# A mixture of experts in 64x64 tiles, with routing over sixteen rounds and its normalisation shared with the next stage

## The chip, the cores and the metric

The kernel runs on one core of one Trainium2 chip. The metric is the device time of one execution in microseconds, the median of several runs.

## The reference

The kernel computes a small language model tower on a batch of 32 sequences of 512 tokens with 64 features: spectral token features, neighbourhood attention, a mixture of experts, a decayed (linear) attention, and a second, softly routed mixture. The change touches the first mixture:

```python
def _moe(tokens, router_w, w1, b1, w2, b2):
    logits = tokens @ router_w.T
    probs = jax.nn.softmax(logits, axis=-1)
    rw, re = jax.lax.top_k(probs, TOP_K)                  # 2 of 8
    rw = rw / jnp.maximum(rw.sum(-1, keepdims=True), 1e-12)
    combine = zeros((N, E)).at[arange(N)[:, None], re].set(rw)
    out = tokens
    for e in range(E):
        h = jax.nn.gelu(tokens @ w1[e] + b1[e], approximate=False)
        y = h @ w2[e] + b2[e]
        out = out + combine[:, e:e + 1] * y
    return out
```

Between the stages the kernel applies the residual and a normalisation over the features (a variance, Ln and Exp for the reciprocal root, and a product).

## The kernel before, in words

**Layout.** Two sequences form a pair: 16 pairs, 64 features of each sequence on 64 of the 128 partitions, 512 tokens along the free axis. `s.h` holds the residual stream, `s.z` the normalised input of a stage. Every stage is a block in which each of the five engines has its own program; they meet at semaphores, and at a barrier between the blocks. Inside a block, `unrolled(count, unroll, (lead, stage), ...)` writes out an engine's order: in iteration n it issues each stage in the order given, for step n + lead.

**The mixture, `mixture_of_experts`.** There are 64 steps: 16 pairs by 4 pairs of experts (`ep`). A step has these parts:

- `first` on TensorE: the four products of two experts by two sequences, 64x64 each, into `p_1` (two PSUM banks).
- `gelu` on ScalarE: one activation of 1024 columns into `g` (two buffers).
- `expand` on TensorE: a 0/1 matrix `s.pick` spreads the routing weights of the step over the partitions of `p_c`, in fp32r and two 32x128 tiles. The weights are held as a high and a low part.
- `weigh` on VectorE: `gw = p_c * g`, 1024 columns.
- `second` on TensorE: two products 128x64 (both experts contracted at once) accumulated into `p_y[slot]`, one bank per pair, with a fp32r bias product at the pair's first step.
- After a pair's last step `residual` on VectorE adds the kept input, and GpSimd adds that into `s.h` and squares it.

TensorE's order per iteration is (4, first), (3, expand), (2, second), (6, turn), (20, logits_of), (0, spreads); ScalarE's is (4, gelu), (6, fetch), (20, router), (0, deviations).

**Routing.** Four pairs are routed together (`router`, once in 16 steps): `logits_of` makes the logits and transposes them into `p_r`, some 20 small VectorE operations follow one another (each waits for the one before) at steps 1 to 7 of the 16, then `turn` transposes the weights into `p_t` and `fetch` copies them to `ct`. For the first group this chain stands ahead of all rounds.

**Normalisation for the next stage.** `spreads` (variance of four pairs, into `p_r`, at step 14 of 16) and `deviations` (copy out; Ln and Exp for three groups together at the third, for the last alone at the end). Then `hop` writes the result to DRAM, `spread` broadcasts a row of it to 64 partitions by two DMAs per pair, and `scaled` on GpSimd makes `s.z`. Of the 16 pairs 12 are scaled at the end of the mixture's block, the last four at the start of `decayed_attention`, which also fetches each pair's halves swapped by two DMAs from SyncE (`fetch`) before it can project. In `decayed_attention` the variances of the following normalisation are made in the bank of the outputs, `p_y`; `outputs` of steps 5, 9 and 13 wait for the Exp that reads it. At the start of the mixture GpSimd scales four pairs, too, before its loop.

**Tables.** ScalarE's function tables are loaded where a function is not in the current set, or ahead with `preload_act_table_set`. The mixture and decayed attention have no such preload.

## Time and profile before

| | |
|---|---|
| median of 3 runs | 962.57 us (961.24 to 964.74) |
| the profiled execution, its own time | 959.21 us |
| its span, first to last instruction | 957.4 us |
| mean granted TensorE clock | 0.931 |
| busy: TensorE products, weight loads | 827.2 us (86%), 414.7 us (43%) |
| busy: VectorE, ScalarE, GpSimd | 570.5 us (60%), 469.8 us (49%), 289.2 us (30%) |
| first mixture, first routing product to barrier | about 390 to 607 us |
| decayed attention | about 607 to 735 us |

PE is TensorE, PEld its weight loads, DVE is VectorE, ACT is ScalarE, POOL is GpSimd, SP is SyncE; q behind an engine means its queue. The start of a row is its time from the start of the span. A row with xN is N instructions merged. Ends of matmuls are modelled, so for TensorE the distance between the starts of neighbouring groups says more than their duration. What stands in brackets is how long the engine was idle before, and which instruction released it. Four f32 products appear as x8, as each is two instructions.

### The profile page before, as it was taken

What the parts mean: (1) busy time and instruction counts of PE and PEld (TensorE: products, weight loads), DVE (VectorE), ACT (ScalarE), POOL (GpSimd) and SP (SyncE); (2) the same over time, 40 slices, a digit from 0 to 9 for tenths busy, and PEclk for the clock granted to TensorE, in tenths of its full rate; (3) what the DMA queues carried; (4) which work ended last, traced back from release to release, by engine and by line L of the source; (5) the groups of instructions that cost most, each with busy time, mean ns of one, the idle gap of its engine ahead of it and who ended that gap; (6) DMA issues with size and microseconds to landing.
All of it is one profiled execution on the core that took longest, in us unless ns stands there. A gap on an engine that the chain in (4) does not pass through costs nothing. (4 is left out here: it accounts for less than half of the span.)

```text
span 957.4 us, 28793 instructions
## 1 busy us (share of the span) xinstructions
PE 827.2 (86%) x12656; PEld 414.7 (43%) x12656; DVE 570.5 (60%) x831; ACT 469.8 (49%) x579; POOL 289.2 (30%) x286
## 2 busy tenths in 40 slices
PE   4796799999999987299999979298886599999996
PEld 2231477767767765022222212176663333333332
DVE  5446477757766765475857525086653147777776
ACT  2243476767767775154444453223332155555553
POOL 4034735334353431311222206533444160000000
PEclk9899799999999999699999979599988689999998
DMA  4200310010010010100000022312322101121110
GB/s 90 31 14 32 97 43 27 4 58 4 4 59 4 4 59 4 55 1 1 1 1 1 1 66 87 101 45 67 89 76 82 26 17 46 56 56 46 45 45 34
DMA packets 39775, 37.81 MB, mean 39 GB/s; under 512 B 21025, under 2 KB 25282, under 8 KB 39650
## 3 DMA queue, kind: packets, MB, share of 16 engines
q1 hardware_dynamic: 38578, 34.35, 12.8%
q8 instruction: 101, 1.65, 0.7%
q10 hardware_dynamic: 1072, 1.60, 0.5%
q14 instruction: 24, 0.20, 0.1%
HBM read 19.95 MB, written 7.60 MB: 29 GB/s over the span
## 5 line engine op out<-in xcount | busy, mean ns | idle before, releaser
L1914 ACT ACTIVATE se_a<-se_p,cols 128x512 f32<-128x512 f32 x128 | 92.7, 774 | 77.5 <-PE se_p L1867 77.5
L1191 DVE TENSOR_REDUCE na_rowmax<-na_ps 128x16 f32<-128x1024 f32 x64 | 78.1, 1220 | 76.8 <-PE na_ps L1067 76.8
L1483 DVE TENSOR_TENSOR me_gw<-me_pc,me_g 128x1024 f32<-128x1024 f32 x64 | 78.3, 1223 | 73.9 <-PE me_pc L1338 69.3
L1934 DVE SCALAR_TENSOR_TENSOR se_a<-se_p,cols,z 128x1024 f32<-128x1024 f32 x64 | 82.2, 1284 | 61.9 <-PE se_p L1877 61.9
L1379 ACT ACTIVATE me_g<-me_p,cols 128x1024 f32<-128x1024 f32 x64 | 71.3, 1114 | 83.9 <-PE me_p L1326 79.2
L925 POOL TENSOR_TENSOR z<-na_k,const 128x512 f32<-128x512 f32 x64 | 64.6, 1042 | 140.7 <-ACT na_k L1131 140.7
L496 POOL TENSOR_TENSOR n_sq<-h 128x512 f32<-128x512 f32 x64 | 68.6, 1077 | 110.3 <-DVE h L848 43.2
L531 POOL TENSOR_TENSOR z<-h,n_bc 128x512 f32<-128x512 f32 x62 | 78.4, 1280 | 24.4 <-DMA n_bc<-n_spread 24.3
L1194 DVE TENSOR_TENSOR na_e<-na_ps,na_rowmax 128x1024 f32<-128x1024 f32 x64 | 78.4, 1225 | 2.2
L1326 PE MATMUL me_p<-z,moe_w 64*64 64x512 f32 x512 | 72.4, 636 | 6.6 <-ACT me_g L1379 6.6
L1867 PE MATMUL se_p<-z,f_w 64*64 64x512 f32 x256 | 70.5, 618 | 4.9 <-DMA se_zswap<-z 4.0
L1076 PE MATMUL na_pt<-const,na_e 128*128 128x128 f32 x512 | 69.2, 278 | 2.3 <-ACT na_et L1161 1.7
L1348 PE MATMUL me_py<-me_gw,w_out 128*64 128x512 f32 x256 | 69.9, 625 | 0.4 <-DVE me_gw L1483 0.4
L1161 ACT ACTIVATE na_et<-na_pt 128x1024 f32<-128x1024 f32 x64 | 65.5, 1024 | 7.7 <-PE na_pt L1076 6.8
L1867 PE MATMUL se_p<-se_zswap,f_w 64*64 64x512 f32 x256 | 69.1, 618 | 0.0
L1877 PE MATMUL se_p<-se_a,f_w 64*64 64x512 f32 x512 | 68.3, 600 | 0.6 <-DVE se_a L1934 0.6
L1154 ACT ACTIVATE na_e<-na_e 128x1024 f32<-128x1024 f32 x64 | 67.3, 1054 | 1.3 <-DVE na_e L1194 0.9
L1889 PE MATMUL se_py<-se_a,w_out 64*64 64x512 f32 x512 | 67.3, 589 | 0.5 <-DVE se_a L1934 0.5
L1265 POOL TENSOR_TENSOR h<-h,me_added 128x512 f32<-128x512 f32 x16 | 20.7, 1292 | 151.7 <-DVE me_added L1491 151.7
L1076 PEld LDWEIGHTS na_pt<-const,na_e 128*128 128x128 f32 x512 | 56.0, 140 | 13.8 <-issue 10.8
L1148 ACT ACTIVATE na_v<-na_pm 64x512 f32<-64x512 f32 x64 | 38.6, 604 | 33.2 <-PE na_pm L1027 32.8
L1067 PE MATMUL na_ps<-z,na_q 32*32 32x256 f32 x2048 | 52.9, 397 | 0.6 <-issue 0.6
(288 smaller groups left out, 1322.0 us busy)
## 6 DMA issues: line engine op xcount, KB each, us to landing
n_bc<-n_spread SPq DMA_DIRECT2D x128, 128.0 KB, 3.0
da_zswap<-z SPq DMA_DIRECT2D x32, 128.0 KB, 2.4
se_zswap<-z SPq DMA_DIRECT2D x32, 128.0 KB, 2.3
out<-se_rows SPq DMA_DIRECT2D x16, 256.0 KB, 2.1
n_spread<-n_rstd SPq DMA_DIRECT2D x13, 256.0 KB, 2.0
const<-in_const ACTq DMA_DIRECT2D x1, 712.0 KB, 6.4
const<-in_const ACTq DMA_DIRECT2D x1, 562.0 KB, 4.0
f_w<-in_L_ffn_W SPq DMA_DIRECT2D x4, 128.0 KB
```

The source lines that it names most:

```text
L496: return nc.gpsimd.tensor_tensor(s.sq[p % 8][:], row(s.h, p), row(s.h, p), ALU.mult)
L531: return eng.tensor_tensor(row(s.z, p), row(s.h, p), s.bc[p % 4][:], ALU.mult)
L1076: mm = nc.tensor.transpose(p_t[:, c, :], e[b][:, 2 * c:2 * c + 2, :].rearrange("p h w -> p (h w)"), const(s, "ident"))
L1191: nc.vector.tensor_reduce(rowmax[b][:], scored, AX, ALU.max).then_inc(s_max, 1)
L1194: nc.vector.tensor_tensor(e[b][:], scored, rowmax[b][:].unsqueeze(2).broadcast_to([128, GROUPS, WIN]), ALU.subtract).then_inc(s_diff, 1)
L1326: mm = nc.tensor.matmul(p_1[half[e2], b, :], s.moe_w1[half[b], 2 * ep + e2, :], row(s.z, at.of(4))[half[b], :], start=True, stop=True, ski ...
L1348: mm = nc.tensor.matmul(p_y[slot][half[b], :], s.moe_w2[:, ep, :], gw[at.k % 2][:, b, :], start=False, stop=(ep == EP - 1), skip_group_che ...
L1379: nc.scalar.activation(g[at.k % 2][:], p_1[:], ACT.Gelu, bias=col(s, "moe_b1", ep)).then_inc(s_g, 1)
L1483: nc.vector.tensor_tensor(gw[at.k % 2][:], p_c[:], g[at.k % 2][:], ALU.mult).then_inc(s_gw, 1)
L1867: mm = nc.tensor.matmul(hidden(at.n, e2)[half[b], :], s.f1_w1[half[e2], 2 * ep + e2, :], z[half[e2], :], start=True, stop=True, skip_group ...
L1914: nc.scalar.activation(a1[at.k % 2][:, e2, :], hidden(at.n, e2)[:], ACT.Relu, scale=col(s, "f1_g1", 2 * ep + e2), bias=col(s, "f1_be1", 2 ...
L1934: nc.vector.scalar_tensor_tensor(out=a2[at.k % 2][:], in0=p_2[:], scalar=col(s, "f1_be2", ep), in1=s.f1_w[:, ep, :].unsqueeze(1).broadcast ...
```

## The change

In the mixture:

- `first` is unchanged in its products, but writes into three single banks (`hidden(n, b)`), 6 steps ahead instead of 4. `gelu` becomes two activations of 512 columns per step, into four buffers that lie in free rows of `s.z`.
- `expand` becomes four 64x64 products in bf16. For this the routing weights are split into three bf16 parts (high, middle, rest) instead of two, and the constant `pick` is twice as wide.
- `second` becomes four 64x64 products in f32 into two banks, one for the even, one for the odd experts; the bias becomes two 64x64 f32 products. A pair's end therefore has two parts: `residual` on VectorE for the first bank, `fetch_odd` on ScalarE, a copy of the second, and two additions on GpSimd.
- `p_t` is gone; the turned weights go through `p_r`, and `fetch` copies them twice (bf16 and f32).
- Routing is spread over steps 2 to 15 of the 16 and starts 24 steps ahead instead of 20. GpSimd scales the four pairs left over from before one at a time in its loop.
- The variances stand at steps 17, 33 and 49 instead of 14, 30, 46 and 62. At step 33 Ln and Exp of groups 0 and 1 are made, and their eight pairs are scaled inside the mixture. Swapped halves of pairs 0 and 1 are fetched there. Groups 2 and 3 (variance of the last, Ln, Exp, hops, eight spreads and scalings) move into `decayed_attention`, the variance, Ln and Exp at its start, the spreads and scalings into its first four steps (`former`).
- Both blocks preload a table on ScalarE. The low and high parts of the bias in f32r and the five GpSimd operations that made them are gone.

```diff
-    s.pick = sb("pick_r", [128, EP, 128], F32R)
+    s.pick = sb("pick_b", [128, 2, EP, 128], BF16)
...
+def fetch_swapped(sp, s, p):
+    half = [slice(0, 64), slice(64, 128)]
+    for x in range(2):
+        sp.dma_start(s.swapped[p % 2][half[x], :], row(s.z, p)[half[1 - x], :]).then_inc(s.n_swapped[p % 2], 16)
...
-        p_1, p_c, p_y, p_t, p_r = ps("p1", [128, 2, T])[0], ps("pc", [128, 2, T])[0], ps("py", [128, T], 2), ps("pt", [128, T])[0], ps("pr", [128, T])[0]
+        p_1, p_c, p_y, p_r = ps("p1", [128, T], 3), ps("pc", [128, 2, T])[0], ps("py", [128, 2, T])[0], ps("pr", [128, T])[0]
...
+        def hidden(n, b):
+            return p_1[(2 * n + b) % 3]
...
             def first(at):
-                te.wait_ge(s_g, done(at.n - 1))
+                te.wait_ge(s_g, done(2 * at.n - 2))
...
             def expand(at):
                 te.wait_ge(s_gw, done(at.n - 1))
                 for b in range(2):
-                    rows = slice((2 * slot + b) * ROUTES, (2 * slot + b + 1) * ROUTES)
-                    mm = nc.tensor.matmul(p_c[:, b, :], s.pick[rows, ep, :], routes[rows, :], start=True, stop=True, skip_group_check=True)
+                    for e2 in range(2):
+                        mm = nc.tensor.matmul(p_c[half[e2], b, :], s.pick[half[b], slot, ep, half[e2]], routes[half[b], :],
+                                              start=True, stop=True, skip_group_check=True)
...
             def second(at):
+                if ep == 0:
+                    te.wait_ge(s_even, done(at.of(4) - 1))
+                    te.wait_ge(s_odd, done(at.of(4) - 1))
+                    for b in range(2):
+                        nc.tensor.matmul(p_y[half[b], b, :], s.moe_b2[half[b], slot, :], routes[half[b], :], start=True, stop=False, skip_group_check=True)
                 te.wait_ge(s_gw, done(at.n))
-                for b in range(2):
-                    mm = nc.tensor.matmul(p_y[slot][half[b], :], s.moe_w2[:, ep, :], gw[at.k % 2][:, b, :], start=False, stop=(ep == EP - 1),
-                                          skip_group_check=True)
+                for e2 in range(2):
+                    for b in range(2):
+                        mm = nc.tensor.matmul(p_y[half[b], e2, :], s.moe_w2[half[e2], ep, :], gw[at.k % 2][half[e2], b, :],
+                                              start=(ep == 0 and b != e2), stop=(ep == EP - 1), skip_group_check=True)
...
-            unrolled(EP * NP, 16, (4, first), (3, expand), (2, second), (6, turn), (20, logits_of), (0, spreads))
+            unrolled(EP * NP, 16, (4, turn), (6, first), (3, expand), (2, second), (AHEAD, logits_of), (0, spreads))
...
+            sc.preload_act_table_set("gelu_and_others")
...
             def gelu(at):
-                sc.wait_ge(s_gw, done(at.n - 2))
-                nc.scalar.activation(g[at.k % 2][:], p_1[:], ACT.Gelu, bias=col(s, "moe_b1", ep)).then_inc(s_g, 1)
+                sc.wait_ge(s_gw, done(at.n - 4))
+                for b in range(2):
+                    nc.scalar.activation(g[at.n % 4][:, b, :], hidden(at.n, b)[:], ACT.Gelu, bias=col(s, "moe_b1", ep)).then_inc(s_g, 1)
+
+            def fetch_odd(at):
+                slot, ep = where(at)
+                if ep == EP - 1:
+                    i = at.of(4)
+                    sc.wait_ge(s_w2, done(at.n))
+                    sc.wait_ge(s_hz, done(2 * (i - 2) + 1))
+                    nc.scalar.activation(odd[slot][:], p_y[:, 1, :], ACT.Copy).then_inc(s_odd, 1)
...
-            unrolled(EP * NP, 16, (4, gelu), (6, fetch), (20, router), (0, deviations))
+            unrolled(EP * NP, 16, (2, fetch_odd), (4, fetch), (6, gelu), (AHEAD, router), (0, deviations))
...
         @block.scalar
         def _(sc):
+            sc.preload_act_table_set("natural_log_exp_and_others")
             give_credits(sc, s_qkd)
+
+            def former():
+                sc.wait_ge(s.n_var, quad(2, LAST))
+                nc.scalar.activation(s.rstd[:, 2, :], s.rstd[:, 2, :], ACT.Ln, bias=s.eps[:])
+                nc.scalar.activation(s.rstd[:, LAST, :], p_y[:], ACT.Ln, bias=s.eps[:]).then_inc(s.n_ln, 1)
+                sc.wait_ge(s.n_ln, 7)
+                nc.scalar.activation(s.rstd[:, 2:4, :], s.rstd[:, 2:4, :], ACT.Exp, scale=-0.5).then_inc(s.n_rstd, 2)
```

## Rows read from the trace of the kernel before

**Rows 1.** Timeline, a steady mixture round: start us, duration, engine, line, [idle before <-releaser]

```profile
436.25 1.09 PE L1326 MATMUL me_p<-z,moe_w 64*64 64x512 f32 x8
...
437.27 0.49 PE L1338 MATMUL me_pc<-me_ct,pick_r 32*128 32x512 f32 x2
437.41 1.11 ACT L1379 ACTIVATE me_g<-me_p,cols 128x1024 f32<-128x1024 f32 x1 [1.34 <-PE me_p L1326]
...
437.70 1.08 PE L1348 MATMUL me_py<-me_gw,w_out 128*64 128x512 f32 x4
437.87 1.23 DVE L1483 TENSOR_TENSOR me_gw<-me_pc,me_g 128x1024 f32<-128x1024 f32 x1 [1.23 <-PE me_pc L1338]
...
438.71 1.09 PE L1326 MATMUL me_p<-z,moe_w 64*64 64x512 f32 x8
```

**Rows 2.** Timeline, a pair's end in the last stage

```profile
837.45 1.05 PE L1877 MATMUL se_p<-se_a,f_w 64*64 64x512 f32 x8
...
838.31 1.06 PE L1889 MATMUL se_py<-se_a,w_out 64*64 64x512 f32 x8
...
839.42 0.60 ACT L1922 ACTIVATE se_odd<-se_py 128x512 f32<-128x512 f32 x1 [0.27 <-PE se_py L1889]
...
841.87 0.75 PE L1900 MATMUL se_pt<-const,se_res 128*128 128x128 f32 x4
```

**Rows 3.** Timeline, TensorE alone, window mask of the neighbourhood attention

```profile
237.63 0.43 PE L1061 MATMUL na_ps<-winmask_b,ident_b 32*32 32x512 bf16 x16
237.85 0.40 PE L1067 MATMUL na_ps<-z,na_q 32*32 32x256 f32 x8
```

**Rows 4.** Timeline, start of the mixture: VectorE's slowest, first transpose, first second product

```profile
395.87 1.44 DVE L1435 TENSOR_TENSOR me_best<-me_best,const 128x256 f32<-128x256 f32 x1
...
405.62 1.12 PE L1317 MATMUL me_pt<-const,me_ctin 128*128 128x128 f32 x4 [11.33 <-DVEq L1477]
...
413.79 1.08 PE L1348 MATMUL me_py<-me_gw,w_out 128*64 128x512 f32 x4
```

**Rows 5.** Timeline, around the deviations of three groups

```profile
552.26 1.58 ACT L1396 ACTIVATE n_rstd<-n_rstd,eps 128x1536 f32<-128x1536 f32 x1
...
559.17 1.99 PE L1326 MATMUL me_p<-z,moe_w 64*64 64x512 f32 x8 [6.44 <-ACT me_g L1379]
```

**Rows 6.** Timeline, the seam between mixture and decayed attention

```profile
595.87 1.08 PE L1348 MATMUL me_py<-me_gw,w_out 128*64 128x512 f32 x4 [0.37 <-DVE me_gw L1483]
...
597.83 1.26 POOL L1265 TENSOR_TENSOR h<-h,me_added 128x512 f32<-128x512 f32 x1 [0.90 <-DVE me_added L1491]
...
599.17 1.04 POOL L496 TENSOR_TENSOR n_sq<-h 128x512 f32<-128x512 f32 x1
...
606.21 0.63 ACT L1398 ACTIVATE n_rstd<-n_rstd 128x512 f32<-128x512 f32 x1
...
607.59 0.42 POOL L1561 MEMSET da_state<- 128x384 f32 x1 [2.48 <-POOLq L1223]
...
617.28 1.11 PE L1602 MATMUL da_pqk<-z,w_in 64*64 64x512 f32 x1 [15.08 <-DMA da_zswap<-z]
```

**Rows 7.** Timeline, decayed attention: queries on ScalarE; variance and outputs on TensorE

```profile
652.04 0.69 ACT L1662 ACTIVATE da_q<-da_pqk,cols 128x512 f32<-128x512 f32 x1 [4.32 <-PE da_pqk L1602]
...
663.59 0.69 ACT L1662 ACTIVATE da_q<-da_pqk,cols 128x512 f32<-128x512 f32 x1 [6.33 <-PE da_pqk L1602]
...
669.18 0.69 ACT L1662 ACTIVATE da_q<-da_pqk,cols 128x512 f32<-128x512 f32 x1 [4.33 <-PE da_pqk L1602]
...
708.49 0.69 ACT L1662 ACTIVATE da_q<-da_pqk,cols 128x512 f32<-128x512 f32 x1 [4.32 <-PE da_pqk L1602]
...
721.01 0.69 ACT L1662 ACTIVATE da_q<-da_pqk,cols 128x512 f32<-128x512 f32 x1 [7.31 <-PE da_pqk L1602]
...
653.00 1.07 PE L503 MATMUL da_py<-n_sq,const 128*32 128x512 f32 x8
657.40 1.47 PE L1634 MATMUL da_py<-da_sm,da_v 128*64 128x128 f32 x16 [3.33 <-ACT n_rstd L1670]
```

More of the change, by code:

```diff
@@ L179, in allocate @@
         "sq", "var", "ln", "rstd", "z", "zero", "hop0", "hop1", "hop2", "hop3")]
+    s.swapped = [s.z[:, NB - 2 + n, :] for n in range(2)]
+    s.n_swapped = [ctx.enter_context(nc.semaphore(f"n_s_swapped{n}")) for n in range(2)]
     s.n_bc = [ctx.enter_context(nc.semaphore(f"n_s_bc{k}")) for k in range(4)]
@@ L250, in later_loads @@
         loads.append((s.raw_bo[n:n + 1, :, :], a["L1_ffn_bo"].rearrange("(p two) d -> two p d", two=2)[e2:e2 + 1]))
-        for pair in range(2):
+        for slot in range(2):
             for part in range(3):
-                r = (2 * pair + e2) * ROUTES + part * NE
-                loads.append((s.raw_moe_b2[r:r + NE, e2, :], a["L0_ffn_b2"]))
+                r = (2 * e2 + slot) * ROUTES + part * NE
+                loads.append((s.moe_b2[r:r + NE, slot, :], a["L0_ffn_b2"]))
         first = (2 * D, D)[e2]
@@ L1153, in stage @@
                     sc.wait_ge(s_diff, done(2 * at.n + b))
[L1154 removed]
+                    nc.scalar.activation(e[b], e[b], ACT.Exp, scale=float(DH) ** -0.5).then_inc(s_e, 1)
                 return stage
@@ L1269, in after @@
                 square(nc, s, p).then_inc(s.n_sq, 1)
-                if p >= 13:
-                    for m in range(4 * (p - 13), 4 * (p - 13) + 4):
-                        pool.wait_ge(s.n_bc[m % 4], spread_done(2, m))
-                        scaled(nc.gpsimd, s, m).then_inc(s.n_z, 1)
             unrolled(NP, 2, (0, after))
@@ L1312, in turn @@
                 if at.k % 8 == 0:
[L1313 to L1318 removed]
+                    c, part = at.of(16), at.k // 8
+                    te.wait_ge(s_ctin, done(c))
+                    if part == 0 and c < LAST:
+                        te.wait_ge(s_route, linked_to(c + 1, 1))
+                    else:
+                        te.wait_ge(s_ct, done(2 * c + part - 1))
+                    if part == 1 and c > 0:
+                        te.wait_ge(s_copied, done(c - 1))
+                    for t in range(4):
+                        mm = nc.tensor.transpose(p_r[:, t * 128:t * 128 + 128], ct_in[:, t, part, :, :, :].rearrange("p b j n -> p (b j n)"), const(s, "ident"))
                     mm.then_inc(s_t, 1)
@@ L1530, in fetch, with former @@
             def fetch(at):
-                k, z = at.k, row(s.z, at.n)
-                sp.wait_ge(s_qk, done(at.n - 2))
-                sp.wait_ge(s.n_z, nth(2, at.n))
-                for x in range(2):
-                    sp.dma_start(swapped[k][half[x], :], z[half[1 - x], :]).then_inc(s_zin[k], 16)
+                if at.n >= 2:
+                    sp.wait_ge(s_qk, done(at.n - 2))
+                    sp.wait_ge(s.n_z, nth(2, at.n))
+                    fetch_swapped(sp, s, at.n)
+            def former(at):
+                if at.n < 4:
+                    for p in (8 + 2 * at.n, 9 + 2 * at.n):
+                        if p == 8:
+                            sp.wait_ge(s.n_rstd, quad(2, LAST))
+                            for n in (2, 3):
+                                hop(sp, s, 2, n)
+                        if p % 4 == 0:
+                            sp.wait_ge(s.n_hop[p // 4], hop_done(2, p // 4))
+                        sp.wait_ge(s.n_z, nth(2, p - 4))
+                        spread(sp, s, 2, p, p // 4)
             def normal(p):
@@ L1548, in after @@
                     normal(at.n - 5)
-            sp.wait_ge(s.n_hop[LAST], hop_done(2, LAST))
-            for p in range(4 * LAST, NP):
-                sp.wait_ge(s.n_z, nth(2, p - 4))
-                spread(sp, s, 2, p, LAST)
-            unrolled(NP, 2, (3, fetch), (0, after))
+            unrolled(NP, 2, (2, fetch), (0, former), (0, after))
             normal(NP - 5)
@@ L1562, in _ @@
             give_credits(pool, s_qd)
-            for p in range(NP - 4, NP):
-                pool.wait_ge(s.n_bc[p % 4], spread_done(2, p))
-                scaled(nc.gpsimd, s, p).then_inc(s.n_z, 1)
             def decayed_queries(at):
@@ L1585, in normal, with former @@
                 scaled(nc.gpsimd, s, p).then_inc(s.n_z, 1)
-            unrolled(NP, 2, (1, decayed_queries), (0, after))
+            def former(at):
+                if at.n < 4:
+                    for p in (8 + 2 * at.n, 9 + 2 * at.n):
+                        pool.wait_ge(s.n_bc[p % 4], spread_done(2, p))
+                        scaled(nc.gpsimd, s, p).then_inc(s.n_z, 1)
+            unrolled(NP, 2, (1, decayed_queries), (0, former), (0, after))
             normal(NP - 6)
```

207 lines of the change are left out of this document (111 added, 96 removed).

## The prediction, as put on record before the result

> **What bounds the kernel now.** I read four views in turn: busy time by stretch, to find the stage that the change rewrites (expert mixture, 390 to 607 us, then decayed attention, 607 to 735); the timeline of one steady round; the waits; and the timeline of the seam between the two stages.
>
> In a steady round TensorE is never free. The first product starts at 436.25, the expansion 1.02 later, the second product 0.43 after that, the next round 1.01 after that: 2.46 us [rows 1]. ScalarE's gelu (1.11) and VectorE's product (1.23) end in time. So only fewer TensorE microseconds, or fewer holes, help here. The same four 64x64 products cost 0.86 where the neighbouring groups are 64x64 too (837.45 to 838.31) [rows 2]; 0.16 of each 1.02 belongs to the change of tile shape. The Trainium skill says so too (TensorEngine Tiling (Array Packing), Key Properties: a change of tiling mode drains the array).
>
> The holes are elsewhere: before the rounds (first transpose at 405.62 behind the routing chain), at the deviations (6.44 idle, then the lower of the two clock levels, 1.2 of 2.4 GHz, a group busy 1.99 instead of 1.09), at the seam (second product 595.87, next projection 617.28, 21.41 us), and at three deviations inside decayed attention [rows 4 to 7].
>
> **The change, part by part.** The sum is made against the profiled execution: span 957.4, its own time 959.2. That is 3.4 below the median of the runs, 962.6, so I carry the difference over to the median.
>
> *A round.* First and second product 0.86 each. The expansion, now bf16 in four 64x64 tiles, streams 512 columns once. The nearest row is the window mask, 16 bf16 tiles of 512 columns, which gives the array up after 0.22 (237.63 to 237.85) [rows 3]. Its upper bound is today's 0.43. I take 0.22, since tile shape no longer changes. Round 1.94. Can the others follow? A first product starting at F reaches gelu at F+1.16 (436.25 to 437.41) [rows 1]; a 512-column activation with a bias takes 0.69 [rows 7]; so the next first product may start at F+1.91. It fits by 0.03. VectorE: expansion to product at most 0.60, then 1.23, under 1.94.
>
> *The copy of the odd half.* Each pair's last second product (start S) is followed on ScalarE by a copy of the second bank. In program order it stands in the same iteration as that product and ahead of a gelu whose first half frees the bank for the next first product. The neighbouring stage's twin starts 1.11 after its product and takes 0.60 [rows 2]. So the gelu's half starts at S+1.71 and ends at S+2.40, and the first product goes at S+2.45 instead of S+0.86: 1.59 idle, for the 14 pairs that still have a first product to come. Queued behind the copy is gelu, behind gelu all of TensorE. A pair is 4 x 1.94 + 0.86 (the bias, f32 now and priced like a group of f32 tiles; if its two tiles overlap the next ones, half of that) + 1.59 = 10.2, against 4 x 2.46 + 0.43 = 10.3 before. The tiles gain 2.1 a pair and the copy and bias take it back.
>
> *Start.* The chain of 20 small VectorE operations runs to 405.5 while GpSimd scales four tiles; three two-input operations are stretched beyond their quiet 0.42, the worst to 1.44 [rows 4], together by 2.5. GpSimd now scales only one tile then. The three-part split adds about 0.5. First transpose at about 403.6: -2.0. Then two copies instead of one (+0.6), but gelu's table is already there and two first products are already made; second product 6.9 after the transpose instead of 8.17: -1.3.
>
> *Second product 0 to 63, before 182.1.* After: 1.7 for the first with its bias; 59 full iterations 114.5; 15 biases 12.9; seven transposes of weights at 0.84 (0.75 busy [rows 2] and a drain) 5.9; two routing products 2.1 (variances and the other transposes fall in the copy's holes); the holes 14 x 1.59 = 22.3; the tail, where no first product covers VectorE, 5.5. The Ln and Exp of two groups still need three table loads: two thirds of Ln's 1.58 and of a like Exp, the copy and the gelu leave TensorE idle 5.2, and then 3.1 are lost at half clock as today after 6.44 [rows 5]: 8.3. Sum 173.2. For routing operations that meet GpSimd's longer work I add 1.5 (between 0 and 10). 174.7: -7.4.
>
> *Seam, before 21.41.* GpSimd starts 1.96 after the last second product; two additions at 1.34 and a square 1.04 end at 5.7; the barrier costs 0.75 (606.84 to 607.59) [rows 6]. The last variance follows, at half clock 1.8, then the projection, whose swapped halves and scaled rows are there: 8.2. Ln, Exp, hop and eight broadcasts are no longer ahead of it: -13.2. What now stands beside the first four pairs: SyncE's 16 broadcasts, GpSimd's two scalings per pair (at 1.26 like its additions, 2.5 of a 5.59 period), ScalarE's Ln and Exp before its first fetch (0.7 late, given back as the variance takes part of the half-clock stretch). I cost these at nothing; without cover they would cost up to 2.5 a pair, 10.
>
> *Decayed attention.* Period 5.59 (663.59 to 669.18), but 11.55 and 12.52 where deviations are made (first and last of three) [rows 7]. TensorE waits 3.33 for Exp and then runs slow. With one table for both, outputs start 1.1 (product to ScalarE, as 436.25 to 437.41) + 0.7 (Ln, like the 0.69) + 0.63 (Exp) + 0.1 = 2.54 after the variance instead of 4.40 (653.00 to 657.40) [rows 1, 6, 7], idle about 1.5. That is less than half of the 3.33 that precedes the slow stretch today, so I take the full clock as kept; if it falls all the same, up to 1.6 come back at each, +5. Saved 5.96 - 2.54 = 3.4 at the first and, taken as the same, at the second, 6.93 - 2.54 = 4.4 at the third: -11.2, and at the last deviations one load, -1.3. The skill's price for a switch (ScalarE: Activation LUTs, What ACT_TABLE_LOAD costs) is about 2.66 with its drain. The trace has the next activation 1.29 after a load's start; by the page each saving would be about twice as large.
>
> Larger constants (256 KB more) land beside preparation, and the five small bias operations leave an idle GpSimd: 0.
>
> Sum: -2.0 -1.3 -7.4 -13.2 -11.2 -1.3 = -36.4. 959.2 - 36.4 = 922.8; on the median, 926.
>
> **The rivals.** *The odd copy hides* (ScalarE gets to gelu first, or three banks suffice): -22.3 more, 904. The order of the stages is against it, the neighbour stage, whose twin is one iteration later and never stalls, is for it only by likeness. *The expansion keeps its 0.43*, or gelu misses its 0.03: up to 62 x 0.21 = +13, 939. *VectorE becomes the bound:* routing now runs beside two additions and a square per pair (3.6 of 10.2 us), each meeting costing up to 1.0 (1.44 against 0.42) [rows 4]; ten two-input operations in each of three sets, a third of them hit, +10, 935. The skill has a mechanism for that (GPSIMD Engine Reference, Specifications: the engines share SBUF interfaces, in contention where VectorE has two SBUF inputs); by it the products with a PSUM input stay at 1.23, as they do here. *Slower than before:* the four bf16 tiles go one after another, 4 x 0.22 instead of 0.22: +0.66 in 62 rounds, +41, 967; it turns the sign from +0.59 a round. The 16 tiles that share 0.22 [rows 3] speak against it. *The preload does nothing* (Ln and Exp still load their own tables in decayed attention): +12, 938; against it stands that the neighbourhood stage, which preloads the same table, shows no load at its Ln and Exp.
>
> **How the numbers follow.** Forecast 926, chance 0.56; copy hidden 0.10; expansion or gelu 0.14; VectorE 0.12; preload idle 0.04; slower 0.04. The range reaches up to the dear expansion and VectorE with a little of both, 944, and down to 908, short of the hidden copy. Outside lie the hidden copy, the slower case and combinations: 2 in 10. 0.3% is 2.9 us: faster 0.95, within 0.01, slower 0.04.
>
> **What would show it.** In the new profile: steady first products 1.94 apart; a hole of 1.6 before the first product after each pair, released by gelu; expansion to second product 0.22; a hole of about 5 at the one Ln in the mixture; last second product to first projection about 8; no table load at Ln or Exp in decayed attention, and 8.1 instead of 11.6 between its queries there. Wrong if the hole is missing (faster), if the round is 2.1 or more, or if TensorE waits for VectorE's products.

## The result, and the profile after

The changed kernel takes 928.4 us (median of four runs, 924.6 to 930.7) against 961.9 for the kernel before in the same comparison: ratio 0.9645, 95% interval 0.9606 to 0.9683. The forecast was 926. The variants further down were measured in three more comparisons, in which the kernel before had medians of 960.9, 962.7 and 963.9. The changed kernel's profiled execution has a span of 925.5 us, 31.9 less than the 957.4 of before, and the parts of that difference can be read off one by one. A "hole" below is a stretch in which TensorE has nothing to do. First a steady round and the end of the first pair.

The timeline of the changed kernel, the last two rounds of pair 0 and the first of pair 1 (start us, duration, engine, line, [idle before <-releaser]):

```profile
417.02 1.06 PE L1368 MATMUL me_py<-me_gw,w_out 64*64 64x512 f32 x8
...
417.88 1.07 PE L1341 MATMUL me_p<-z,moe_w 64*64 64x512 f32 x8
...
418.74 0.42 PE L1353 MATMUL me_pc<-me_ct_parts,pick_b 64*64 64x512 bf16 x4
418.95 1.06 PE L1368 MATMUL me_py<-me_gw,w_out 64*64 64x512 f32 x8
...
420.09 0.60 ACT L1409 ACTIVATE me_odd<-me_py 128x512 f32<-128x512 f32 x1 [1.74 <-PE me_py L1368]
...
420.58 1.26 ACT L1401 ACTIVATE z<-me_p,cols 128x512 f32<-128x512 f32 x2
...
421.31 1.09 PE L1341 MATMUL me_p<-z,moe_w 64*64 64x512 f32 x8 [1.29 <-ACT z L1401]
```

Against [rows 1]: expansion to second product 0.21 instead of 0.43, second to first 0.86 instead of 1.01, first to expansion 0.86 instead of 1.02; second to second 417.02 to 418.95 is 1.93 instead of 2.46. Then the hole: gelu is held by the odd copy, and the first product comes 2.36 after the second (418.95 to 421.31), 1.50 more than 0.86.

The waits of the changed kernel's TensorE between 409 and 575 us (waiting line, releaser: us in total, times, longest). Of the 17 for gelu, 14 stand at the ends of pairs, two in the first rounds, and the 5.0 at the logarithm:

```profile
PE me_p L1341 <- ACT z L1401: 20.4, 17, 5.0
PE me_pc L1353 <- DVE me_gw L1530: 3.0, 2, 2.0
```

Timeline of the start, from the first routing product (TensorE, and the ScalarE operations that it waits for). It answers to [rows 4], where the transposes stood at 405.62 and the second product at 413.79:

```profile
391.80 1.94 PE L1312 MATMUL me_pr<-z,w_in 128*32 128x512 f32 x8 [3.10 <-PEq L877]
...
399.62 0.23 ACT L1394 ACTIVATE me_gap<-me_gap 128x32 f32<-128x32 f32 x1 [5.23 <-DVE me_gap L1485]
399.76 0.58 ACT L1391 ACTIVATE me_logits_t<-me_pr 128x512 f32<-128x512 f32 x1
...
401.44 1.98 PE L1341 MATMUL me_p<-z,moe_w 64*64 64x512 f32 x8
...
404.23 1.98 PE L1341 MATMUL me_p<-z,moe_w 64*64 64x512 f32 x8 [0.81 <-ACT z L1401]
...
406.14 1.11 PE L1331 MATMUL me_pr<-const,me_ctin 128*128 128x128 f32 x4
...
412.33 0.65 PE L1368 MATMUL me_py<-me_gw,w_out 64*64 64x512 f32 x2
```

Timeline of the seam, for [rows 6]. GpSimd goes from its last addition to the square and the barrier, and behind the last variance the projection waits for nothing:

```profile
586.28 1.09 PE L1368 MATMUL me_py<-me_gw,w_out 64*64 64x512 f32 x8 [0.53 <-DVE me_gw L1530]
...
591.00 1.04 POOL L481 TENSOR_TENSOR n_sq<-h 128x512 f32<-128x512 f32 x1
...
593.14 1.94 PE L488 MATMUL da_py<-n_sq,const 128*32 128x512 f32 x8 [5.77 <-PEq L1214]
595.01 1.99 PE L1662 MATMUL da_pqk<-z,w_in 64*64 64x512 f32 x8
```

Timeline of a normalization inside the decayed attention, for [rows 7]; no table load stands between the keys and the logarithm, or between it and the exponential:

```profile
630.10 0.69 ACT L1732 ACTIVATE da_q<-da_pqk,cols 128x512 f32<-128x512 f32 x1 [4.33 <-PE da_pqk L1662]
...
632.18 0.69 ACT L1738 ACTIVATE n_rstd<-da_py,eps 128x512 f32<-128x512 f32 x1 [0.82 <-PE da_py L488]
632.90 0.63 ACT L1740 ACTIVATE n_rstd<-n_rstd 128x512 f32<-128x512 f32 x1
...
633.68 1.09 PE L1696 MATMUL da_py<-da_sm,da_v 128*64 128x128 f32 x16 [1.56 <-ACT n_rstd L1740]
...
638.31 0.69 ACT L1732 ACTIVATE da_q<-da_pqk,cols 128x512 f32<-128x512 f32 x1 [4.78 <-PE da_pqk L1662]
```

The balance, from the starts of such rows (us; of before, of after, difference, forecast):

| stretch | before | after | measured | forecast |
|---|---|---|---|---|
| begin to first routing product | 390.53 | 391.80 | +1.27 | 0 |
| to first transpose | 15.09 | 14.34 | -0.75 | -2.0 |
| to second product 0 | 8.17 | 6.19 | -1.98 | -1.3 |
| second product 0 to 63 | 182.08 | 173.95 | -8.1 | -7.4 |
| seam | 21.41 | 8.73 | -12.7 | -13.2 |
| projection to last exponential | 116.45 | 105.58 | -10.9 | -12.5 |
| last exponential to end | 223.67 | 224.91 | +1.24 | 0 |
| sum | | | -31.9 | -36.4 |

The first and the last row can't be told from the scatter of executions. The variants of the changed kernel, with the same code ahead of the first routing product, took 390.6 to 394.2 us to get there. The second and the third row belong together: from the first routing product to the second product 0 it is 20.53 instead of 23.25, where 19.96 was forecast.

### The profile page after: what moved, and what is told of

Read it like the earlier page. It is cut to its first block and busy times, and to the rows that moved or that the text cites. A ratio compares the mean times of both kernels' runs of the same rounds, so it can differ in the third digit from the quotient of the medians.

```text
span 925.5 us, 29817 instructions
## 1 busy us (share of the span) xinstructions
PE 807.1 (87%) x13088; PEld 423.2 (46%) x13088; DVE 573.1 (62%) x843; ACT 476.7 (52%) x657; POOL 308.8 (33%) x297
## 3 DMA queue, kind: packets, MB, share of 16 engines
q1 hardware_dynamic: 38578, 34.35, 13.3%
## 5 line engine op out<-in xcount | busy, mean ns | idle before, releaser
L1530 DVE TENSOR_TENSOR me_gw<-me_pc,z 128x1024 f32<-128x1024 f32 x64 | 78.3, 1224 | 62.5 <-PE me_pc L1353 41.5
L1401 ACT ACTIVATE z<-me_p,cols 128x512 f32<-128x512 f32 x128 | 80.9, 685 | 44.2 <-PE me_p L1341 39.7
L1341 PE MATMUL me_p<-z,moe_w 64*64 64x512 f32 x512 | 82.8, 626 | 21.2 <-ACT z L1401 21.2
L1368 PE MATMUL me_py<-me_gw,w_out 64*64 64x512 f32 x512 | 90.0, 601 | 0.5 <-DVE me_gw L1530 0.5
L1178 DVE TENSOR_TENSOR z<-na_ps,na_rowmax 128x1024 f32<-128x1024 f32 x64 | 78.4, 1225 | 2.2
L1060 PE MATMUL na_pt<-const,z 128*128 128x128 f32 x512 | 69.9, 280 | 2.3 <-ACT na_et L1145 1.7
L1138 ACT ACTIVATE z<-z 128x1024 f32<-128x1024 f32 x64 | 67.4, 1054 | 1.3 <-DVE z L1178 0.9
L1060 PEld LDWEIGHTS na_pt<-const,z 128*128 128x128 f32 x512 | 56.6, 142 | 13.7 <-issue 10.9
L1270 POOL TENSOR_TENSOR h<-h,me_even 128x512 f32<-128x512 f32 x16 | 21.3, 1331 | 119.3 <-DVE me_even L1538 119.3
L1132 ACT ACTIVATE na_v<-na_pm 64x512 f32<-64x512 f32 x64 | 38.5, 602 | 32.3 <-PE na_pm L1011 31.9
L1077 PE MATMUL na_po<-na_v,na_et 128*32 128x18 f32 x4096 | 49.7, 188 | 3.0 <-issue 2.1
```

The lines of the kernel that those rows point to most:

```text
L1060: mm = nc.tensor.transpose(p_t[:, c, :], e[b][:, 2 * c:2 * c + 2, :].rearrange("p h w -> p (h w)"), const(s, "ident"))
L1178: nc.vector.tensor_tensor(e[b], scored, rowmax[b][:].unsqueeze(2).broadcast_to([128, GROUPS, WIN]), ALU.subtract).then_inc(s_diff, 1)
L1341: mm = nc.tensor.matmul(hidden(at.n, b)[half[e2], :], s.moe_w1[half[b], 2 * ep + e2, :], row(s.z, at.of(4))[half[b], :], start=True, stop= ...
L1368: mm = nc.tensor.matmul(p_y[half[b], e2, :], s.moe_w2[half[e2], ep, :], gw[at.k % 2][half[e2], b, :], start=(ep == 0 and b != e2), stop=(e ...
L1401: nc.scalar.activation(g[at.n % 4][:, b, :], hidden(at.n, b)[:], ACT.Gelu, bias=col(s, "moe_b1", ep)).then_inc(s_g, 1)
L1530: nc.vector.tensor_tensor(gw[at.k % 2][:], p_c[:], g[at.n % 4], ALU.mult).then_inc(s_gw, 1)
```

## The experiments

Every run below was made beside the kernel before; times are medians. Stretches are those of the table, taken from each run's trace.

**1. The odd copy behind the gelu.**

```diff
-unrolled(EP * NP, 16, (2, fetch_odd), (4, fetch), (6, gelu), (AHEAD, router), (0, deviations))
+unrolled(EP * NP, 16, (4, fetch), (6, gelu), (2, fetch_odd), (AHEAD, router), (0, deviations))
```

> The changed kernel with one line of ScalarE's order changed: the odd copy is issued behind the gelu of the same step instead of ahead of it; nothing is left out. In the changed kernel's trace TensorE's first products wait for a gelu that was held up by the odd copy (start to start 2.36 instead of 0.86 us, so 1.50 at each of 14 places, 21 in all). If the odd copy on ScalarE is the cause of that hole, it shrinks to some 0.3 us and the kernel takes about 911 us (905 to 916). Rival one, the odd copy is needed as early as it is, by the routing product that turns it: the wait moves there and the time stays within 3 us of 928. Rival two, VectorE is the next bound: about half comes back, 919 to 923.

Measured 920.4 us, ratio to before 0.9569 (0.9525 to 0.9614); second product 0 to 63: 165.2 us, 8.8 less than the 173.95 of the changed kernel. Waits of TensorE in this run, same stretch:

```profile
PE me_pc L1353 <- DVE me_gw L1530: 6.2, 4, 2.9
PE me_p L1341 <- ACT z L1401: 6.1, 3, 4.7
```

The cause is confirmed: 17 waits for gelu become 3 (the logarithm's and the two of the first rounds), so all 14 at the ends of pairs are gone, and the period across a pair's end goes from 3.47 to 2.24 in nine of them. The size is that of rival two. The intervals of this ratio and of the changed kernel's just overlap, so the size is taken from the stretch, which took 173.95, 174.26 and 174.15 in three traces with the changed kernel's mixture (its own, experiments 5 and 8). The rest of the gain goes to two things. The smaller one is TensorE's own work: at three pair ends (4, 8 and 12) the period falls only to 3.11, since the variances that had stood inside the hole are now in the open:

```profile
464.40 1.06 PE L488 MATMUL me_pr<-n_sq,const 128*32 128x512 f32 x8
```

The larger one is VectorE: at three places, one for each routing in the mixture, the waits move to it. Its timeline at the first of them:

```profile
435.84 1.21 DVE L1530 TENSOR_TENSOR me_gw<-me_pc,z 128x1024 f32<-128x1024 f32 x1
436.97 0.28 DVE L1510 CAST me_high<-me_weights 128x256 bf16<-128x256 f32 x1
437.28 1.17 DVE L1513 TENSOR_TENSOR me_weights<-me_weights,me_high 128x256 f32<-128x256 f32 x1
438.38 1.35 DVE L1514 CAST me_ctin<-me_high 128x256 f32<-128x256 bf16 x1
...
439.86 1.21 DVE L1530 TENSOR_TENSOR me_gw<-me_pc,z 128x1024 f32<-128x1024 f32 x1
```

Weighing follows weighing after 4.02 where a round takes 1.93: the 2.9 us between 436.97 and 439.86 are routing work. My rivals had VectorE and the odd copy as alternatives. They are in series: the copy's hole covered most of what VectorE was late by (the fourth wait of the view is the short one at the mixture's end).

**2. Expansion in 32x128 tiles again, bf16 kept.**

```diff
-for e2 in range(2):
-    mm = nc.tensor.matmul(p_c[half[e2], b, :], s.pick[half[b], slot, ep, half[e2]], routes[half[b], :], ...)
+rows = slice((2 * b + slot) * ROUTES, (2 * b + slot + 1) * ROUTES)
+mm = nc.tensor.matmul(p_c[:, b, :], s.pick[rows, slot, ep, :], routes[rows, :], ...)
```

> The changed kernel with the expansion alone taken back to two bf16 products of 32 rows by 128 columns for each round; the first and second products stay 64 by 64. If it is the change of the tile shape between expansion and the products around it that cost the round its 0.33 us before, the round goes from 1.93 to about 2.27 us and the kernel from 928 to about 946 us (940 to 950; less than 62 times 0.33 where a wait for gelu already held TensorE). If only the number of products or their number format counted, the time stays within 3 us of 928.

Measured 939.9 us, 0.9763 (0.9707 to 0.9819); second product 0 to 63: 188.7 us, 14.7 more. TensorE's timeline in the steady rounds:

```profile
416.90 1.04 PE L1341 MATMUL me_p<-z,moe_w 64*64 64x512 f32 x8
417.87 0.39 PE L1353 MATMUL me_pc<-me_ct_parts,pick_b 32*128 32x512 bf16 x2
418.19 1.09 PE L1367 MATMUL me_py<-me_gw,w_out 64*64 64x512 f32 x8
```

The round is 2.20, 0.27 more than 1.93: first to expansion 0.97 (was 0.86), expansion to second 0.32 (was 0.21), and 0.05 in second to first. The tile shape costs about 0.11 at each change here, less than the 0.16 that I had read out of [rows 2] and expected. From expansion to second product the kernel before took 0.43, this one 0.32, the changed one 0.21. The second 0.11 is the expansion's shape. The first goes with the number format and with the second product's own shape, which no run takes apart. More than the format counted, so the rival is out; the 11.5 to 14.7 us stay under the expected 18, since a round gives 0.27 and not 0.33, and some fall in the holes.

**3. No logarithm and exponential in the mixture.** Two copies of 32 columns stand in their place, so this kernel leaves out that part of the normalization and its result is not the reference's.

```diff
-nc.scalar.activation(s.rstd[:, 0:2, :], s.rstd[:, 0:2, :], ACT.Ln, bias=s.eps[:]).then_inc(s.n_ln, 1)
+nc.scalar.activation(s.rstd[:, 0:2, 0:32], s.rstd[:, 0:2, 0:32], ACT.Copy).then_inc(s.n_ln, 1)
```

(and the exponential likewise)

> The changed kernel with the logarithm and the exponential of the first two groups' variances inside the mixture replaced by two copies of 32 columns each, which leaves that part of the normalization out and its two changes of ScalarE's function table with it. The priced hole is 5.2 us of idle TensorE and 3.1 us of half clock after it. If the table changes make it: about 920 us (918 to 922), and no second product at half clock in the middle of the mixture. Rival, the hole belongs to the variances and the router that stand in the same place: only the two operations' own 1 to 2 us come back, 926 to 927.

Measured 919.0 us, 0.9560 (0.9502 to 0.9618); second product 0 to 63: 168.55 us, 5.4 less. The pair with the logarithm, from its first second product to the next pair's, takes 17.82 us in the changed kernel and 10.86 here: the table loads and the half clock behind them are worth 7.0 (forecast 8.3), the two operations' own time included. 1.6 of it are lost again in the pair behind (14.06 instead of 12.50), where a first product runs at half clock (1.93) that has the full clock in the changed kernel (1.03); whether the edit brings that about is not shown. The longest wait of TensorE for gelu falls from 5.0 to 1.3. The median's 9.4 is more than the 5.4 of the mixture. 3.4 of the rest lie after the last exponential, where nothing was changed (221.5 us to the end instead of 224.9).

**4. The kernel before with one table load at the head of the decayed attention.**

```diff
 def _(sc):
+    sc.preload_act_table_set("natural_log_exp_and_others")
     give_credits(sc, s_qkd)
```

> The kernel before with one instruction more: the function table that holds both logarithm and exponential is loaded once at the head of the decayed attention, and nothing else is changed. By the trace of before, each of the table changes there lay open on the chain (two of 1.28 to 1.29 us for each of four normalizations, and one ahead of the last exponential): 8 to 9 times 1.28, so 10 to 12.5 us less than the kernel before, 950 to 953 us. Rival one, the load is redone by each function anyway: no change, within 1 us of 962. Rival two, by what the Trainium skill's page ScalarE: Activation LUTs gives for a table load with its drain (2.66 us) the gain would be twice as large, 940 us.

Measured 945.3 us, 0.9829 (0.9778 to 0.9880). From the first queries to the last 91.25 us instead of 101.68, and each of the three long periods 8.22 instead of 11.55, 11.36 and 12.52: -10.4, and -1.3 at the last exponential. These are the changed kernel's own periods to 0.01 us. So this one instruction makes all that the change gains there, and the scalings, hops and broadcasts moved in from the mixture cost nothing. The rest is not of the chain. The profiled execution is 16.8 shorter, 11.7 of it here; 3.2 lie behind the last exponential (220.5 us to the end against 223.7), 1.3 ahead of the first routing product and 1.2 in one slow round of the mixture (180.87 us from second product 0 to 63 against 182.08), all in code that is the same. The expectation's sum was right, but its mechanism was not: what a load costs a period is read in experiment 8.

**5. The second logits' copy ahead of the tanh.**

```diff
-if at.k == 0:
+if at.k == 0 and c != 1 or at.n == 9:
+    c = 1 if at.n == 9 else c
```

> The changed kernel with ScalarE's copy of the second routing's logits issued ahead of the first routing's tanh, not behind it; nothing is left out. Theory: in the changed kernel that copy (399.76) stands behind a tanh that waits for VectorE (399.62), TensorE's transposes of the logits wait for the copy 2.31 us with the first products behind them, and the second first product (404.23) is then still running when the parts of the first routing can be turned (406.14). With the copy ahead, the transposes of the logits start near 398.9, the first products 1.5 us earlier, and the turn follows the router's last operation at once: from the first routing product to the turn 13.0 to 13.3 us instead of 14.34. Rival: the turn waits for the router's own chain on VectorE and stays at 14.2 to 14.4. The whole time says nothing at this size.

Measured 929.2 us (one run). TensorE's timeline at the start:

```profile
399.51 1.99 PE L1341 MATMUL me_p<-z,moe_w 64*64 64x512 f32 x8
...
405.46 1.08 PE L1331 MATMUL me_pr<-const,me_ctin 128*128 128x128 f32 x4 [1.18 <-DVE me_logits L1464]
406.47 1.99 PE L1341 MATMUL me_p<-z,moe_w 64*64 64x512 f32 x8
409.27 1.99 PE L1341 MATMUL me_p<-z,moe_w 64*64 64x512 f32 x8 [0.81 <-ACT z L1403]
```

The order works as meant: first products 1.6 us earlier against the first routing product, and the turn no longer stands behind them. But it still comes 14.00 after the first routing product (14.34 before the edit), not 13.0 to 13.3: it waits 1.18 for VectorE's copy of the second logits, which stands behind the whole chain of the first routing. It has to: `p_t` is gone, the turned weights go through `p_r`, and `p_r` holds the second logits until they are copied out. That is the rival but for 0.2. And the two first products behind it run at half clock, so the second product comes 8.25 after the turn instead of 6.19. Nothing is gained.

**6. The routing operations spread, on top of the first experiment.** VectorE's routing steps 6 to 14 each go one round earlier, and the split begins so:

```diff
-if at.k == 14:
+if at.k == 13:
     linked(v.tensor_copy(high[:], weights[:]))
     ...
     linked(v.tensor_tensor(weights[:], weights[:], high[:], ALU.subtract))
+if at.k == 14:
     v.tensor_copy(parts[:, :, :, :, 0:NE], by_place(high))
```

> The odd copy behind the gelu, as in the first experiment, and VectorE's routing operations spread more evenly: the masked step joins the one before it, and the split of the weights into parts starts one round earlier, so that its four first operations lie in two rounds instead of one; nothing is left out. Theory: in the first experiment the rest of the gain was lost at three places, where the split (3.9 us in one round, stretched beside GpSimd) kept the weighing, and so the expansion, waiting; measured against its neighbours each such place costs 2.5 to 4.5 us, 10 in all. Spread out, half or more of that comes back: 5 us less than the first experiment, so 913 to 917. Rival: the stretching beside GpSimd takes whatever stands there, and the time stays within 2 us of 920.

Measured 916.6 us, 0.9528 (0.9485 to 0.9571); second product 0 to 63: 160.96 us, 4.2 less than in the first experiment. The worst period of each place (4.02, 2.93 and 5.14 there) is 2.41 here. The three pairs with a routing took 9.9 us more than their neighbours in the first experiment, 5.7 of it TensorE's waits for VectorE. Of that cost less than half came back: the operations are still as long where GpSimd's work meets them (the subtraction 1.40 instead of 0.43, the next cast 1.16 instead of 0.29).

**7. The scalings of the first eight pairs, and the first two swapped loads, behind the seam.** The lines (hops and broadcasts too) are moved from the mixture's GpSimd and SyncE programs to the head of those of the decayed attention:

```diff
-if 10 <= p < 14:
-    rescale(2, 2 * (p - 10))
-    rescale(2, 2 * (p - 10) + 1)
...
+for p in range(8):
+    pool.wait_ge(s.n_bc[p % 4], spread_done(2, p))
+    scaled(nc.gpsimd, s, p).then_inc(s.n_z, 1)
```

> The changed kernel with one part of the seam undone: the broadcasts and scalings of the first eight pairs, and the swapped loads of the first two, are made at the head of the decayed attention instead of inside the mixture (their logarithms and exponentials stay in the mixture); nothing is left out. The change took the seam from 21.41 to 8.73 us. Theory: the seam was the chain hop, broadcast, scaling, swapped load behind the deviations, of which this puts back everything but the squares, variance and deviations: a hop, a broadcast, a scaling and a swapped load of 2 to 2.4 us each (1.5 for the scaling) less what the variance of the last group covers, so project comes 5 to 7 us later, and the kernel takes 934 to 937 us. Rival: those steps are hidden behind the last group's variance and the table load, as the transfers before were not the bound, and the time stays within 2 us of 928.

Measured 933.9 us, 0.9720 (0.9667 to 0.9772). The timeline at the seam (SPq is SyncE's DMA queue):

```profile
589.79 0.80 SPq L494 DMA_DIRECT2D n_spread<-n_rstd  x2
...
591.81 6.20 SPq L506 DMA_DIRECT2D n_bc<-n_spread  x10
...
598.05 1.24 SPq L1207 DMA_DIRECT2D z<-z  x2
...
601.36 1.99 PE L1662 MATMUL da_pqk<-z,w_in 64*64 64x512 f32 x8 [8.84 <-DMA z<-z]
```

The seam is 17.64 us, 8.9 longer. My sum had left SyncE's queue out: five pairs' broadcasts take 6.20 us to issue, and the swapped load that projection waits for stands behind them. The mixture takes 171.8 us, 2.2 less (GpSimd has eight scalings less there). The time is 5.5 up on the changed kernel's: inside what was expected of the step, though the seam by itself is more. So having the rows ready ahead of the seam is worth 8.9 there against this order. It is no share of the 12.7 that the change gained, since the kernel before had these rows scaled inside the mixture, too. What its projection waited for was the swapped load, and that stood in SyncE's queue behind the last group's eight broadcasts, which waited for the last Exp (ended at 606.84):

```profile
608.89 5.11 SPq L521 DMA_DIRECT2D n_bc<-n_spread  x8
...
614.11 2.61 SPq L1535 DMA_DIRECT2D da_zswap<-z  x4
```

The change gained by taking both out of the way: the first swapped loads are made in the mixture, and the last group's deviations and broadcasts come behind the first projection. How the 12.7 divide between the two no run shows.

**8. The changed kernel without the load of experiment 4.**

> The changed kernel without the one load of the function table at the head of the decayed attention; nothing is left out. If the preload is what made each normalization's extra time fall there to 2.62 us, and the broadcasts and scalings that were moved into the decayed attention are hidden, this gives back what the preload took off the kernel before (10.4 us between the first and the last queries and 1.3 behind them by the traces): 938 to 942 us, with the three long periods at 11.5 us or more again. Rival: the scalings that are there now cover the loads, and less than half comes back, 928 to 933.

Measured 937.3 us, 0.9756 (0.9698 to 0.9814). The periods are 11.55, 12.79 and 11.54 again; first queries to last exponential 114.14 us instead of 103.10, +11.0. ScalarE at the first of them:

```profile
631.09 1.28 ACT L1737 ACT_TABLE_LOAD   x1
632.39 0.69 ACT L1737 ACTIVATE n_rstd<-da_py,eps 128x512 f32<-128x512 f32 x1
633.09 1.28 ACT L1739 ACT_TABLE_LOAD   x1
634.39 0.63 ACT L1739 ACTIVATE n_rstd<-n_rstd 128x512 f32<-128x512 f32 x1
```

And TensorE behind them:

```profile
635.16 1.67 PE L1696 MATMUL da_py<-da_sm,da_v 128*64 128x128 f32 x16 [3.33 <-ACT n_rstd L1739]
636.76 1.65 PE L1700 MATMUL da_py<-da_qd,da_state 128*128 128x128 f32 x6
```

A load takes 1.30, from its start to that of the activation behind it. But of the first, 0.82 is hidden: that long ScalarE sits idle for the variance in the changed kernel. So TensorE waits 3.33 instead of 1.56, 1.77 more (2 x 1.30 - 0.82 = 1.78), and the other 1.56 of the period's 3.33 come behind the wait: the two groups of outputs run slow (1.67 and 1.65 instead of 1.09 and 0.94), since the granted clock is down behind the long wait and not behind the short one. The windows of 6 us behind the wait have it at 0.72 here (635 to 641) and in the kernel before (657 to 663), and at 1.00 in the changed one (633 to 639).

**9. The second product in 128x64 tiles again.** One bank for a pair, no odd copy, no second addition.

```diff
-for e2 in range(2):
-    for b in range(2):
-        mm = nc.tensor.matmul(p_y[half[b], e2, :], s.moe_w2[half[e2], ep, :], gw[at.k % 2][half[e2], b, :], ...)
+for b in range(2):
+    mm = nc.tensor.matmul(p_y[half[b], slot, :], s.moe_w2[:, ep, :], gw[at.k % 2][:, b, :], ...)
```

> The changed kernel with the second product alone taken back to two products of 128 rows by 64 columns for each round into one bank for each pair: the second bank, the odd copy and GpSimd's second addition go with it; nothing is left out. Theory: each pair's 64 by 64 tiles save two changes of tile shape at some 0.16 us in each of its four rounds (1.3 in all), and the odd copy that they need costs a hole of 1.50 and the wider bias some 0.4; so a pair takes 4 times 2.26 and one bias of 0.43 to 0.86, 9.5 to 9.9 us, instead of 10.1, and the kernel takes 919 to 927 us: what the second product's tiles gain, their copy has taken back. Rival: the second product's tiles are worth their 0.33 in each of 62 rounds and the hole stays, since ScalarE is late for another reason: 940 to 949.

Measured 924.6 us, 0.9593 (0.9550 to 0.9636), 3.8 below the changed kernel. TensorE's timeline:

```profile
416.66 1.09 PE L1338 MATMUL me_p<-z,moe_w 64*64 64x512 f32 x8
417.57 0.40 PE L1350 MATMUL me_pc<-me_ct_parts,pick_b 64*64 64x512 bf16 x4
417.89 1.08 PE L1363 MATMUL me_py<-me_gw,w_out 128*64 128x512 f32 x4
418.90 1.09 PE L1338 MATMUL me_p<-z,moe_w 64*64 64x512 f32 x8
```

The round is 2.24, and a pair is 9.84 (three rounds and 3.10 with the bias) against 10.1. Second product 0 to 63 takes 171.4 us, 2.6 less, and the seam 7.36, 1.4 less for the addition that is gone. By the traces this part of the change is a loss of 4 us as it was made: 0.31 gained in each round, and more than that handed back once per pair. The medians alone could not tell it, since the intervals of the ratios overlap; the stretch and the seam can, since three traces with the changed kernel's mixture agree to 0.3 (experiment 1), and its seam is 8.73 or 8.78 wherever its code is unchanged.

**10. Both tables loaded by hand inside the mixture.** Logarithm and exponential's ahead of the one, gelu's behind the other.

> The changed kernel with two instructions more: inside the mixture the table that holds both logarithm and exponential is loaded ahead of the one logarithm, and gelu's behind the exponential; nothing is left out. Theory: of the three table loads there, one (1.28 us) goes, and gelu's starts without waiting for the next gelu's input; TensorE's longest wait (5.0) falls to 3.7 or less, 1.3 to 2.6 us less in the mixture, 926 to 927 by the median, which is inside the noise of one comparison, so the trace decides. Rival: each function still loads its own table, and the wait stays at 5.0.

Measured 926.8 us, 0.9613 (0.9570 to 0.9657), which can't be told from 928.4. The trace has two table loads there instead of three and the longest wait at 3.8 instead of 5.0; the two rounds take 11.89 instead of 12.43. The mixture as a whole gains nothing in this execution (174.97 us from second product 0 to 63 against 173.95): as in experiment 3, the pair behind takes 14.06 instead of 12.50, with a group at half clock.

**11. Experiments 1, 6 and 10 together.**

> The changed kernel with the odd copy behind the gelu, the routing operations spread, and the two table loads of the run before it; nothing is left out. If the three add up: 916.6 for the first two together less 1.3 to 2.6, 914 to 915.5. If the long wait at the logarithm is hidden or replaced once the other holes have moved, 916 to 917.

Measured 912.2 us over six runs, 0.9464 (0.9424 to 0.9503): 16 us below the changed kernel and the fastest of all. Second product 0 to 63 is 159.66 us (160.96 in experiment 6). The pair with the logarithm takes 14.83 us instead of 16.97, so here the load by hand shows. The median is about 2 us better than the sum, which this measurement can't tell from it.

## Why the prediction was right

**The round** held: 1.94 forecast, 1.93 measured, and the bf16 expansion 0.21 for 0.22. The experiments split its 0.53: about 0.27 come with the expansion's tile shape, 0.31 with that of the second product (either edit puts a change of shape between expansion and second product, so the two overlap). The rivals of a serial expansion and of gelu missing its 0.03 are out: past the first rounds no product inside a pair waits for gelu, but for the one at the logarithm.

**The odd copy** held: 1.59 forecast, 1.50 measured, and the waits for gelu between 409 and 575 us are 17 with 20.4 us, the logarithm's 5.0 among them. That it costs this much was the step that kept the forecast of the rounds at -7; the first experiment shows the copy as its cause, and the ninth that the whole second-product part is worth less than nothing with it. The bias, put at 0.86, is 0.89 (10.11 for a pair, less four rounds and 1.50). The logarithm's hole, put at 8.3 with the half clock behind it, is 7.0 (experiment 3).

**VectorE** was priced at 1.5 between bounds of 0 and 10. In the changed kernel TensorE waits for it twice, 3.0 us in all, which is what the prediction had named as a sign of being wrong; in the first experiment it is 5.7 at three places, in pairs that cost 9.9 more than their neighbours. That the term came near was luck: the odd copy's hole hid the rest.

**The seam** held (8.2 forecast, 8.73 measured; from GpSimd's square to the variance it is 1.10, where the barrier had been put at 0.75), and so did the claim that the work moved beside the first pairs is hidden (experiment 4 against the changed kernel, 8.22 and 8.21).

**The deviations** came to 8.21 where 8.13 was forecast. By the price that the Trainium skill gives for a load with its drain (ScalarE: Activation LUTs, What ACT_TABLE_LOAD costs: about 2.66) two loads would have been 5.3 in a period; the trace has 1.30 for each, and the measurement decides. The stretch is 1.6 short of forecast. 0.9 is the last variance, at half clock in this execution (1.93 instead of 1.06, where experiments 4 and 8 have the full clock on the same code), 0.4 the three periods (10.8 saved where 11.2 was forecast, since the second had been taken as equal to the first), 0.43 the former logarithms ahead of the first queries, which I had put at 0.7 and given back.

**The start** was mis-sized: -0.75 instead of -2.0 to the turn. GpSimd's contention is gone as I had it (all two-input operations at 0.42 to 0.50), and VectorE's chain was done at 404.9. The step that failed is what comes behind it. I had costed the early first products at nothing, and in this execution they stood in the turn's way at half clock (404.23, 1.98). Without that, the turn would still have waited for the second logits, as experiment 5 shows; in experiment 8, where the clock rose in time, the interval is 13.91 with no edit at this place, and the turn waits 0.30 for VectorE's copy. So 0.4 of the 1.25 are the clock's, and 0.8 a link that my sum did not have: with `p_t` gone the turned weights need `p_r`, and have to wait until the second logits have left it. The next term erred the other way, -1.98 to the second product where -1.3 was forecast.

**The sum** was 4.5 us too hopeful on the spans, -31.9 against -36.4. 2.5 of it lie before the first routing product and after the last exponential, within the scatter of executions: the last stretch took 223.7 in the trace of before and 220.5 in experiment 4 on the same code. What stays open is why those stretches differ between executions beyond what the clock rows say; I made no experiment on it.

## What to carry to other kernels

Price a new tile shape together with the buffers it asks for: the second product's tiles saved 0.31 us a round and cost 1.5 a pair, by one copy that stood ahead of a gelu in an engine's program order; one line changed in that order gave back 8.8 us in the mixture, more than going back to the old tiles. When a hole goes, look at the engine that was late behind it before counting the hole as gain: of 14 holes of 1.5 us, 21 in all, 8.8 came back, and 4.2 more only after the next engine's work was spread. Two functions that share a table want one load by hand where they alternate in a stage: here one instruction was worth 11 us, half of it through the clock that the shorter waits kept up.

## What the runs showed of the hardware

- **Executions differ at fixed places, and the clock with them.** The same instructions from the first routing product to the second product 0 took between 19.57 us (experiment 8, where the second first product already runs in 1.09) and 21.51 (experiment 3, where it takes 1.99), and 20.53 in the changed kernel. Behind the last exponential the same work took 220.5 to 225.3 us. These windows of before, of the changed kernel and of experiment 4, each from 14 to 15 us behind its last exponential, show the granted clock beside it (us, busy time of PE, PEld, DVE, ACT, POOL, granted clock, DMA share, GB/s); their stretches to the end were 223.7, 224.9 and 220.5:

```profile
748.00:763.00 15.00, 10.77 (x46) 8.42 (x46) 2.35 (x7) 3.21 (x6) 0.32 (x1) 0.70 0.00 1
```

```profile
715.00:730.00 15.00, 11.36 (x47) 9.00 (x46) 2.36 (x7) 3.21 (x6) 0.00 (x0) 0.66 0.00 0
```

```profile
735.00:750.00 15.00, 9.10 (x44) 6.64 (x48) 1.78 (x4) 2.99 (x5) 3.44 (x3) 0.84 0.13 30
```

- **GpSimd stretches casts too.** A VectorE cast of 256 bf16 columns to f32, one input, took 0.29 in the changed kernel's quiet start and 1.35 beside one of GpSimd's scalings (experiment 1, 438.38), as much as two-input operations; the weighing, with one input in PSUM, stayed at 1.21 to 1.23.
- **bf16 and f32 products alternate for nothing** inside one tile shape (expansion to second product 0.21, a quarter of the f32 groups' 0.86, and those take 0.86 beside a bf16 group as beside each other), while a change of shape cost 0.11 to 0.16.
